# A vision tower in one kernel: the sine table ahead of the pixels, VectorE's complex product of group 0 ahead of the layer norm of group 3, and new orders up to the feed-forward part

## The reference, cut to what matters

```
h = patches(x)                                # 36 patches of 768 per image
h = layernorm(h)*ln1_w + ln1_b ; h = h @ W + b ; h = layernorm(h)*ln2_w + ln2_b
h = concat(cls, h) + pos                      # 37 tokens of 192 per image
# state space block: LN3, RMS norm, input product, causal conv and scan, output product
xn = gamma * rms(layernorm(h)); xp = xn @ W_in.T + b_in
y  = scan(conv(xp), sigmoid(A), sigmoid(Bp), sigmoid(C)) ; h = h + y @ W_out.T + b_out
# feed-forward: patches 6.. through gelu(. @ W1 + b1) @ W2 + b2, tokens 0..5 through pairs of experts
h = h + ffn(layernorm(h))
```

## Time and profile before

| | |
|---|---|
| median of 3 runs | 98.2 us (97.67 to 98.42) |
| profiled execution, its own time | 99.03 us |
| span in the profile | 97.3 us |
| TensorE busy | 85.5 us, 88% |
| VectorE busy | 60.9 us, 63% |
| ScalarE, GpSimd busy | 38.7 and 41.1 us |
| DMA | 13.59 MB, two thirds of the way at 200 to 320 GB/s |

### The profile page before, as it was taken

One profiled execution on the slowest core, in us unless ns is written; L12 is line 12 of the kernel. 1 busy time (PEld: TensorE's weight loads), 2 busy tenths in 40 slices (PEclk: granted clock), 3 DMA queues, 4 the chain that ended last, 5 costly groups with the idle time before them and its releaser, 6 DMA issues.

```text
span 97.3 us, 1841 instructions
## 1 busy us (share of the span) xinstructions
PE 85.5 (88%) x579; PEld 71.0 (73%) x579; DVE 60.9 (63%) x209; ACT 38.7 (40%) x105; POOL 41.1 (42%) x112
## 2 busy tenths in 40 slices
PE   5997599999988978969999989969899999999940
PEld 5995399989966758757588889956577726888830
DVE  4659999547999999999976993573100307038410
ACT  0620957562345644104492053420964204870000
POOL 6525799998974230538746005353500400000000
PEclk9999999999999999999999999999999999999996
DMA  1999998497628994699999921010202100000211
GB/s 14 262 259 255 257 275 150 87 259 175 194 67 268 322 214 136 109 281 235 246 326 314 292 68 41 17 46 13 78 20 81 34 28 11 0 0 0 63 52 39
DMA packets 16294, 13.59 MB, mean 140 GB/s; under 512 B 5907, under 2 KB 14332, under 8 KB 16284
## 3 DMA queue, kind: packets, MB, share of 16 engines
q1 hardware_dynamic: 14860, 13.39, 52.0%
q10 hardware_dynamic: 1424, 0.08, 1.2%
HBM read 12.43 MB, written 1.04 MB: 138 GB/s over the span
## 4 chain that ended last, share of the span: by engine, by line
PE 55%; DVE 24%; DMA 7%; ACT 4%; ACTq 3%; issue 3%; DVEq 0%
PE ps L1184 50%; DMA ssm<-in_L_attn_C_dram 7%; DVE h L994 3%; DVE xT_area L1027 2%; DVE xs L1012 2%; DVE xT_area L1030 2%; PE ps L1208 2%; DVE st L1000 2%; DVE h L977 2%; DVE st L967 2%; ACT x4TT L654 2%; DVE xT_area L1036 1%; ACT xT_area L654 1%; DVE ag L969 1%; DVE Y L1036 1%
## 5 line engine op out<-in xcount | busy, mean ns | idle before, releaser
L1184 PE MATMUL ps<-W_area,xT_area 128*108 128x192 f32 (+2 forms) x72 | 13.7, 329 | 1.5 <-ACT xT_area L654 1.3
L1184 PEld LDWEIGHTS ps<-W_area,xT_area 128*108 128x108 f32 (+2 forms) x72 | 10.9, 170 | 2.3 <-issue 2.1
L1184 PE MATMUL ps<-W_sb,pixel_area 128*124 128x192 f32 x48 | 8.8, 332 | 0.0
L1184 PEld LDWEIGHTS ps<-W_sb,pixel_area 128*124 128x124 f32 x48 | 7.7, 187 | 1.2 <-issue 1.2
L1184 PE MATMUL ps<-WoutT,xT_area 128*108 128x192 f32 (+1 forms) x42 | 7.6, 328 | 1.0 <-DVE xT_area L1036 1.0
L1184 PEld LDWEIGHTS ps<-WoutT,xT_area 128*108 128x108 f32 (+1 forms) x42 | 6.8, 177 | 1.4 <-DVE xT_area L1036 1.4
L1184 PE MATMUL ps<-dM,WinT 128*128 128x216 f32 (+2 forms) x36 | 7.2, 335 | 0.0
L1184 PE MATMUL ps<-x4TT,W_sb 128*128 128x248 f32 x24 | 6.1, 387 | 1.1 <-ACT x4TT L654 1.1
L654 ACT ACTIVATE xT_area<-ps,ln_col 128x576 f32<-128x576 f32 (+1 forms) x6 | 4.9, 809 | 4.5 <-PE ps L1208 4.5
L1184 PEld LDWEIGHTS ps<-dM,WinT 128*128 128x128 f32 x36 | 5.8, 190 | 0.8 <-issue 0.8
L1184 PE MATMUL ps<-warm_sb 128*128 128x128 f32 x24 | 5.4, 412 | 1.1 <-DVE warm_sb L863 1.1
(11 more groups left out here) (212 smaller groups left out, 197.3 us busy)
## 6 DMA issues: line engine op xcount, KB each, us to landing
line_area<-in_L_ffn_A_W_dram SPq DMA_DIRECT2D x5, 576.0 KB, 9.4
A_sb<-in_L_ffn_A_W_dram SPq DMA_DIRECT2D x5, 384.0 KB, 4.3
pixel_area<-in_x_dram SPq DMA_DIRECT2D x6, 288.0 KB, 7.1
A1R<-in_L_ffn_A_W_dram SPq DMA_DIRECT2D x10, 96.0 KB, 3.6
W_area<-in_L_tok_W_dram SPq DMA_DIRECT2D x2, 288.0 KB, 5.6
W_sb<-in_L_ffn_moe_W_dram SPq DMA_DIRECT2D x1, 576.0 KB, 8.2
W_sb<-in_L_ffn_moe_W_dram SPq DMA_DIRECT2D x1, 384.0 KB, 5.9
W1R<-in_L_ffn_moe_W_dram SPq DMA_DIRECT2D x2, 192.0 KB, 5.7
```

What stands on the lines that cost most here:

```text
L1184: return t.matmul(out_, lhsT, rhs, start=start, stop=stop, skip_group_check=True)
```

## The change

It reorders all five lists between the start and the first `up`, and adds little:

- **Loads.** LN1's weight and bias are loaded as four rows (`ln1_rows`) in place of columns. TensorE transposes them (three transposes after `warm(10)`), and VectorE copies them to `ln1_col`. Each half of the token weights comes in two DMAs, channel 0 apart from channels 1 and 2. The two loads of W_out stand behind the small loads.
- **VectorE at the start.** Three memsets go to GpSimd; six short instructions for `eps_rows` and two memsets go in between the `bn_stats`. All of the sine table up to the third coefficient stands ahead of the first pixels, the rest right behind; `F` stands ahead of the `bn_stats`. The row sum (`fold_rows`) stands ahead of the three `ms1T` products.
- **GpSimd.** Its memsets stand ahead of the second `line_up`, chunk 5's `line_up` one step later; `pads` and `perm` later; `add_cls` ahead of `root2(4)`.
- **TensorE.** Groups 0 and 1 get all their six products before the LN1 statistics are turned; then groups 2 and 3; the transposes of W_in and of W_out's third part stand behind. The other two parts of W_out are turned into bank 5 behind the first pair's input product. The class correction stands behind `project_out(1)` and `transform(4)`. `turn_x4(0)` and `turn_x4(1)` stand ahead of `invert(2)`, `turn_x4(1)` goes to bank 5, and `project_out(4)` waits for the copy of it. The first `up` is cut into six images and two (`up_first`), and `turn_x4(4)` and `(5)` stand between its halves.
- **ScalarE.** Its copies follow these orders; `put_x4T(1)` stands ahead of `put_P(4)`.
- **VectorE in the block.** `multiply(0)` stands ahead of `spread(3)`, `multiply(1)` behind `normed(3)`, `center(4)` behind that; `normed(5)` ahead of `multiply(2)`.

```diff
@@ loads (SP, ACT)
+            load_W(0, 0)
             load_x(0, 1)
+            load_W(1, 0)
             load_x(1, 0)
+            load_W(0, 1)
             load_x(1, 1)
+            load_W(1, 1)
...
-            act.dma_start(ln1_col[:, 0], ln1_w.rearrange("(h p c) -> p h c", h=H2, c=NC)).then_inc(l_ln1, 16)
+            act.dma_start(ln1_rows[0:H2, :], ln1_w.rearrange("(h q) -> h q", h=H2)).then_inc(l_ln1, 16)
...
@@ scalar
             a_.activation(table_row[:, 1:2], ones[:, 0:1], ACT.Sqrt)
-            put_xT(1)
             act.dma_start(gcol[:, 0:1], gamma[0:DL].unsqueeze(1)).then_inc(l_gam, 16)
...
+            put_xT(1)
             line_up(2)
-            put_xT(2)
             act.wait_ge(t_gT, 1)
...
+            put_xT(2)
             line_up(4)
             put_xT(3)
             put_xT(4)
+            put_xT(5)
...
@@ vector, start
+            k = step(v.tensor_scalar(tb_n[:, :, :], tb_s[:, :, :], COEF[6], None, MUL))
+            for c in COEF[5:3:-1]:
+                dve.wait_ge(vec_step, k)
+                k = step(v.scalar_tensor_tensor(tb_n[:, :, :], tb_n[:, :, :], c, tb_s[:, :, :], ADD, MUL))
             dve.wait_ge(l_x[0][0], 16)
...
+            dve.wait_ge(t_ln1, 1)
+            v.tensor_scalar(ln1_col.rearrange("p i h c -> p c i h"),
...
+            for c in COEF[3:0:-1]:
...
@@ vector, block
             normed(2)
+            multiply(0)
             spread(3)
+            normed(3)
+            multiply(1)
             center(4)
-            normed(3)
-            multiply(0)
-            multiply(1)
...
             spread(5)
+            normed(5)
             multiply(2)
-            normed(5)
@@ tensor
+            pe.wait_ge(l_ln1, 32)
+            for c in range(NC):
+                ins = t.transpose(ps[:, 7, 2 * H2 * c:2 * H2 * (c + 1)],
+                                  ln1_rows.rearrange("p (q c) -> p c q", c=NC)[:, c], ident[0:2 * H2, 0:2 * H2])
+            ins.then_inc(t_ln1, 1)
...
-            product(0, [0, 1, 2])
+            product(0, [0, 2])
             turn(1)
-            product(0, [3, 4, 5])
-            product(1, [0, 1, 2])
-            turn(2)
+            product(0, [3, 1, 4, 5])
             pe.wait_ge(tab_ready, 1)
...
-            product(1, [3, 4, 5])
+            product(1, [0, 1])
+            turn(2)
+            product(1, [2, 3])
             turn(3)
-            product(2, [0, 1, 2, 3])
+            product(1, [4, 5])
+            product(2, [0, 1])
             turn(4)
-            product(3, [0, 1, 2, 3])
             turn(5)
+            product(3, [0, 1])
             product(4, [0, 1])
+            product(5, [0, 1])
...
-            project_in_pair(0)
+            project_in_even(0)
+            project_in_odd(0)
+            pe.wait_ge(h_free, 4)
+            turn_Wout(0, 5, 0)
+            turn_Wout(1, 5, D).then_inc(t_w, 1)
             transform(2)
             transform(3)
...
+                if g == 4:
+                    pe.wait_ge(x4T_ready, 2)
...
+            turn_x4(0)
+            turn_x4(1)
             invert(2)
-            turn_x4(0)
             project_out(4)
-            turn_x4(1)
...
+            up_first()
             turn_x4(4)
             turn_x4(5)
+            up_rest(0)
```

More of the change, by code:

```diff
@@ L244, in vit_tower_kernel @@
         l_x = [[sem(f"l_x{c}{hh}") for hh in range(H2)] for c in range(NC)]
-        l_tokW = [sem(f"l_tokW{hh}") for hh in range(H2)]
+        l_tokW = [[sem(f"l_tokW{hh}{k}") for k in range(2)] for hh in range(H2)]
+        t_ln1, ln1_ready, pool_zero = sem("t_ln1"), sem("ln1_ready"), sem("pool_zero")
         l_Win, l_Wout, l_G, l_A1, l_A1b, l_A2, l_A2b, l_W1, l_W2 = [sem(f"l_{n}") for n in (
@@ L567, in _ @@
                     ins.then_inc(K_ready, 1)
-            g_.memset(hid_par[:, :, :, CT // 2:], 0.0).then_inc(pads_ready, 1)
-            for j in range(2):
-                g_.tensor_scalar(perm[:, :, :, j],
-                                 ident[:, 64 * j:64 * j + CT // 2].rearrange("p (i b) -> p i b", b=NB),
-                                 1.0, 1.0, MUL, MUL).then_inc(perm_ready, 1)
             def residual_scales(g):
@@ L618, in add_cls @@
                 g_.tensor_tensor(u_rep[:, :, CLS], u1[:, 0, :], bK[:, :, 0], ADD).then_inc(u_ready, 1)
+            root2(2)
             residual_scales(0)
-            root2(2)
+            root2(3)
             residual_scales(1)
-            root2(3)
+            g_.memset(hid_par[:, :, :, CT // 2:], 0.0).then_inc(pads_ready, 1)
+            for j in range(2):
+                g_.tensor_scalar(perm[:, :, :, j],
+                                 ident[:, 64 * j:64 * j + CT // 2].rearrange("p (i b) -> p i b", b=NB),
+                                 1.0, 1.0, MUL, MUL).then_inc(perm_ready, 1)
             residual_scales(2)
+            residual_scales(3)
+            add_cls()
             root2(4)
-            residual_scales(3)
             root2(5)
-            add_cls()
             add_ob(0)
@@ L701, in _ @@
             a_.activation(ms1[:, :, 2], ms1[:, :, 1], ACT.Sqrt, bias=eps5[0:BH, :]).then_inc(rs1_ready, 1)
-            put_xT(5)
-            act.wait_ge(l_gam, 48)
-            act.wait_ge(t_w, 1)
-            copy(WinT[:, :], ps[:, 6, 0:E], scale=gcol[:, 0:1]).then_inc(wT_ready, 1)
             act.wait_ge(F_ready, 4)
@@ L934, in _ @@
                     step(v.bn_stats(st1[:, nw, c, :], x_pix[:, c, :, nw, :]))
+            dve.wait_ge(ident_ready, 1)
+            step(v.tensor_reduce(eps_rows[:, 0:1], ident[0:ST, 1:ST:4], AX.X, ADD))
+            k = step(v.tensor_reduce(eps_rows[:, 1:2], ident[0:ST, 3:ST:4], AX.X, ADD))
+            dve.wait_ge(vec_step, k)
+            k = step(v.tensor_scalar(eps_rows[:, 1:2], eps_rows[:, 1:2], EPS5, None, MUL))
+            dve.wait_ge(vec_step, k)
+            k = step(v.tensor_tensor(eps_rows[:, 0:1], eps_rows[:, 0:1], eps_rows[:, 1:2], ADD))
+            dve.wait_ge(vec_step, k)
+            dve.wait_ge(pool_zero, 3)
+            step(v.tensor_scalar(fold_rows[0:ST, D:D + 1], eps_rows[:, 0:1], EPS5, None, MUL))
+            v.memset(xcR[:, 3], 0.0).then_inc(pads_ready, 1)
+            v.memset(xcL[:, 3], 0.0).then_inc(pads_ready, 1)
             for hh in range(H2):
@@ L1276, in _ @@
             fold([0, 1])
-            product(3, [4, 5])
-            turn_Win_rest()
+            product(3, [2, 3])
             product(4, [2, 3])
@@ L1429, in _ @@
             project_out(0)
-            project_in_pair(1)
+            project_in_even(1)
+            project_in_odd(1)
+            project_out(1)
+            transform(4)
             pe.wait_ge(u_ready, 2)
@@ L1435, in _ @@
             ins.then_inc(t_ob, 1)
-            project_out(1)
-            transform(4)
             invert(0)
@@ L1455, in _, with up @@
             turn_x4(3)
-            def up(s, js, last):
+            def up(s, js):
                 for j in js:
@@ L1463, in up, with up_first, up_rest @@
                     mm(upslot(s, j), W1_sb[:, m * 128:(m + 1) * 128], x4TT[:, 0, b0:b0 + nb, NCLS:T], j < 2, False)
-                if not last:
-                    return
+            def up_first():
+                for b0, nb, n in ((B0[0], NBG[0] + NBG[2], 3), (B0[3], NBG[3], 4)):
+                    pe.wait_ge(x4T_ready, n)
+                    for j in range(4):
+                        m = STEPS[0][j][1]
+                        mm(upslot(0, j)[:, NPT * b0:NPT * (b0 + nb)], W1_sb[:, m * 128:(m + 1) * 128],
+                           x4TT[:, 0, b0:b0 + nb, NCLS:T], j < 2 and n == 3, False)
+            def up_rest(s):
                 for j in range(4):
```

161 lines of the change are left out of this document (78 added, 83 removed).

## The result

The kernel became slower. Median of 4 runs 101.94 us (100.45 to 103.82), against 97.94 us for the kernel before, measured beside it (97.6 to 98.42); the ratio is 1.026, with an interval of 1.017 to 1.035. I had forecast 96.9 us, 95.3 to 98.8. The profiled execution took 100.45 us, its span 98.7 us.

A forecast was written before the change was run, and what follows sets the result against it. TensorE, busy 88% of the span, was taken as the bound. Leads of 2.4 us at the first complex product, 0.3 at `project_out(0)` and 1.1 at `invert(1)` ended at 1.3; 98.2 - 1.3 = 96.9 us, range 95.3 to 98.8.

The forecast's parts named there:

- VectorE comes to the pixels some 0.3 us late: At the start: table instructions ahead of the first pixels, less the memsets and `eps_rows` that leave, delay VectorE 0.3 us.
- the seven steps at 0.25 us each: At the start: seven short sine table instructions ahead of the first pixels, priced at about 0.25 us each.
- New overlaps with GpSimd's work I put at nothing net: VectorE in the block, before `invert(1)`: no net cost from new overlaps; one more stretched instruction would be 0.7 us.
- Rival 3: TensorE's clock falls in the new 2.7 us gap at 33 us, adding 2.4 us: 99.3 us, slower; chance 0.10.
- a gap of 2.7 us ahead of `transform(3)`: TensorE has used up its cover at 33.0 and stands 2.7 us, waiting for `xs` of group 3 behind `multiply(0)`.
- the roots uncovered: ScalarE's two roots ahead of `normed(3)`, no longer covered by other work: 0.45 us in all.
- 2.1 us of the 2.4 us lead given back: From first complex product to `project_out(0)`: VectorE's new order leaves 0.3 of the 2.4 us lead.
- rival 2: At the start: the loads land no sooner, 1.4 us of gain is gone: 98.3 us, no change; chance 0.15.
- `invert(1)` was ended by `norm4`: Sign of being right: TensorE's wait at `invert(1)` ends with VectorE's `norm4`; forecast at 48.25, 1.1 us ahead.
- The new wait of `project_out(4)`: Behind `invert(2)`: `project_out(4)` waits for ScalarE's copy of x4T of group 1, costing 0.5 us.
- 0.76 and 0.13 less 0.5: Before the first `up`: 0.76 us wait gone, 0.13 back from `turn_x4(1)` moved ahead, 0.5 cost at `project_out(4)`.
- The step from the profile to the median: Whole kernel: the median of the runs taken as 0.83 us below the profiled execution, giving 96.9 us.

The follow-up runs named there:

- the late zeroing: Changed kernel with only GpSimd's zeroing of `fold_rows`, `ms1T` and `G` moved behind the second `line_up`: 99.13 us, ratio 1.007.
- and old order: Changed kernel with that zeroing moved behind the second `line_up` and VectorE's block order of before for groups 0 to 3, no filler: 96.12 us, ratio 0.984.
- the old-order run: Changed kernel with only VectorE's block order of before for groups 0 to 3 (`multiply(0)` behind `normed(3)`): 98.17 us, ratio 0.998.
- the kernel before with the new order: Kernel before with only VectorE's new order for groups 0 to 3 (`multiply(0)` ahead of `spread(3)`): 102.23 us, ratio 1.038.
- the warming alone: Changed kernel with six more matmuls on constants ahead of `turn(0)`: 99.73 us, ratio 1.012.
- the pixels first: Changed kernel with VectorE's copy of its half of chunk 0 moved in front of the sine table's steps: 101.95 us, ratio 1.024.
- The filler ahead of `transform(3)`: Ten unused matmuls on constants between `transform(2)` and `transform(3)`: changed kernel 101.02 us, ratio 1.011; with the late zeroing 98.53 us, ratio 1.004.
- the late table without the old order: Changed kernel with only the sine table's polynomial put back behind the pixels and the first copy out of PSUM: 102.49 us, ratio 1.028.
- the old x4 places: Changed kernel with block order of before, six warming matmuls, and `turn_x4(0)`, `turn_x4(1)` and ScalarE's copies where they stood before: 96.24 us; zeroing moved too: 95.99 us.

## Why the prediction was wrong

The milestones on TensorE, in us of the span, from the rows of each run; the last two columns are the changed kernel with the late zeroing, and the same with the old order in the block.

| | before | predicted | after | zeroing late | and old order |
|---|---|---|---|---|---|
| statistics turned | 19.68 | 17.8 to 17.9 | 20.20 | 18.20 | 18.01 |
| `project_out(0)` | 36.93 | 36.6 | 38.92 | 36.92 | 34.66 |
| `invert(1)` | 49.33 | 48.25 | 51.04 | 48.87 | 46.62 |
| first `up` | 64.51 | 63.05 | 65.77 | 63.60 | 61.35 |
| span | 97.3 | 96.0 | 98.7 | 96.5 | 94.3 |

The stretches between them show where the sum failed: in the first alone by more than half a microsecond (predicted 17.85 us, measured 20.20), hardly at all in the second, which holds the new order of VectorE.

| stretch | before | predicted | after | zeroing late | and old order |
|---|---|---|---|---|---|
| to the turned statistics | 19.68 | 17.85 | 20.20 | 18.20 | 18.01 |
| to `project_out(0)` | 17.25 | 18.75 | 18.72 | 18.72 | 16.65 |
| to `invert(1)` | 12.40 | 11.65 | 12.12 | 11.95 | 11.96 |
| to the first `up` | 15.18 | 14.80 | 14.73 | 14.73 | 14.73 |

**The step that failed first** is "VectorE comes to the pixels some 0.3 us late". It was 1.9 us (6.84 against 4.90). I had priced the seven steps at 0.25 us each, and had not laid GpSimd's list beside them, though the change puts its memsets ahead of the second `line_up`. Four steps were stretched, by 0.65 (L888), 0.14, 0.24 and 0.89 us (L898, L900, L902); without these 1.92 us VectorE would have come at 4.92. The row that I took the price from had the cause in it: the 1.83 us for five steps are four of 0.23 us and one of 0.77, which began at 8.52, just behind GpSimd's `line_up(1)` at 8.38. I read the mean of 0.37 as the wait for the result; with GpSimd idle, three steps of the same kind took 0.76 us. "New overlaps with GpSimd's work I put at nothing net", with 0.7 us for one more of the kind, was the right mechanism, asked only of the block. The Trainium skill (SBUF — State Buffer, "Who interferes with whom") says that a VectorE instruction in a two-port mode, or one with two inputs in SBUF against a GpSimd instruction that reads SBUF, and a GpSimd instruction exclude each other for the whole instruction, by who starts first. The rows agree, as far as they go: L902 has one input and was held up by zeroings (which mode it ran in no row shows), while L905, with two inputs, ran its two steps in 0.50 us beside a zeroing in the old-order run, and the steps of L918 took 1.39 us there beside a copy and 0.76 us without.

**What it set off** I had not thought of: TensorE stood idle for 1.29 us ahead of `turn(0)` and 0.71 us ahead of `product(0)`, and its clock fell at 9 us. Turned statistics came 2.3 us behind the forecast although VectorE had them ready at 17.94. With the late zeroing `product(0)` began at 7.90 (I had said 0.4 us behind 7.57) and the statistics came at 18.20, 0.3 us off. The move is worth 2.8 us in the medians, of the 5.0 by which I was off, and by the ratios half of the error (1.026 became 1.007; the forecast was 0.987).

**Rival 3**, the clock falling in the gap of 2.7 us, came true in the profiled run and stood at 0.10, which was too low. Its price of 2.4 us was for 5.8 us at half pace, and what the profiles show is less. The dip from 39.7 to 43.1 us withholds half of 3.4 us, 1.7, but from `project_out(0)` to `invert(1)` the kernel after took only 0.17 us more than with the late zeroing (12.12 and 11.95): in the latter TensorE waits 1.02 us for `norm4` at the end of this stretch, and a slower TensorE only uses that wait up. A fall of 6.8 us cost more: 1.5 us by the spans in the kernel before with the new order, and with the warming alone 1.6 us from the turned statistics to `invert(1)` (32.25 against 30.67). And the rival covered one gap where there were two. The clock did not fall in every execution: not in the profiles with the pixels first and with the late zeroing, at gaps of 2.53 and 2.54 us. The filler ahead of `transform(3)` was worth 1.5% in the changed kernel by the two ratios, 0.2% with the late zeroing (0.6 us by the medians). Why the second is so much less no run isolates.

**The order in the block** I had right: a gap of 2.7 us ahead of `transform(3)` (2.55), VectorE's idle time ahead of `multiply(0)` 1.7 us (1.51), the roots uncovered (0.46), 2.1 us of the 2.4 us lead given back (2.06). From the turned statistics to `project_out(0)` I had 18.75 us, and it took 18.72. It was the largest single loss in the sum, and that it was counted right is why the error lies elsewhere.

**The rest.** The loads landed early enough: the sigmoid waited for nothing, and rival 2 was wrong. `invert(1)` was ended by `norm4` once the start was right, as said, at 48.87 against 48.25; the stretch ahead of it was 0.3 us longer than my terms, and which of them was short no run shows. The new wait of `project_out(4)` was 0.54 us (0.5), and the first `up` had none. The dense end was as long as before. From `invert(1)` to the first `up` 15.18 us before became 14.73, a gain of 0.45 where my terms give 0.39 (0.76 and 0.13 less 0.5).

**The step from the profile to the median** failed too. The profiled execution of before stood 0.83 us above its median, and I took that off. The profile after is the fastest of its four runs, 1.5 us under its median, and that with the late zeroing is the fastest of ten, 98.28 us, with a median of 99.13. So even the kernel nearest to my prediction, whose span is within 0.5 us of the forecast, is 0.7% slower than before by the ratio and 1.0% by the medians. Part of that may be a clock that falls in some executions: the ten ran at mean granted clocks of 0.960 (99.79 and 99.87 us) to 1.000, the three at 0.998 or more took 98.28 to 98.59, and with the filler ahead of `transform(3)` all ten stood at 0.992 or more and none took over 98.94. That is a hint and no proof, since in the run with the filler alone one of 101.15 us has a mean of 0.998.

**What remains to be had.** The old order in the block with the rest of the change and the zeroing moved gives 96.12 us against 97.89, 1.6% under the kernel before by the ratio. With the warming, the old x4 places and either place of the zeroing it is 96.0 us, the best that was run.

## What to carry to other kernels

Before moving steps on VectorE, lay GpSimd's list of the same microseconds beside them, memsets included: the price of a short step is then not its own but the rest of GpSimd's instruction. Price each new idle stretch of TensorE twice, as a wait and as a clock that may fall behind it, and ask it of the start as well as of the place that the change is about. Filler matmuls on constants are a cheap way to tell the two apart. And ask what comes behind the fall: here a dip that withheld 1.7 us of work cost 0.17 us, since TensorE would have waited for VectorE anyway.

## What the runs showed of the hardware

A VectorE addition on 24 elements took 2.42 us beside a GpSimd addition of 2.03 us, where the same instruction took 0.23 us in the kernel after and 0.22 with the old order alone. It began 0.4 us ahead of that addition, while GpSimd's instruction before it was still running (until 17.72), so when that one ended GpSimd's next went ahead of it. L902 in the kernel after shows the same: it began beside the zeroing of `fold_rows`, and ended only behind the two that followed.

The granted clock fell at 9 us in the kernel after, with idle times of 1.29 and 0.71 us just before, where the kernel before kept it through one of 1.32 us and one of 0.50. Behind a gap of 2.5 us in the block it fell in three profiles (the kernel after, the warming alone, the late table without the old order) and stayed up in two (the pixels first, the late zeroing). The Trainium skill (TensorE: Matmul & The Clock Gate, "HAM oscillation — how this bites in real kernels") puts such falls down to idle gaps of TensorE; the trace agrees in kind, and shows that gaps of one size don't always bring one.
